# Self attention of the first stage: another order of its work, heads in alternating halves, the context copy ahead of the reciprocal root

## The reference

```python
x = x + _L0_xattn_ref(_layernorm(x, axis=-1), ctx_768, Wq, Wk, Wv, Wo, bo)

# inside, with h = 8 heads of d = 64
q = (x @ Wq).reshape(B, Sq, h, d).transpose(0, 2, 1, 3)
k = (context @ Wk).reshape(B, -1, h, d).transpose(0, 2, 1, 3)
v = (context @ Wv).reshape(B, -1, h, d).transpose(0, 2, 1, 3)
scores = jnp.einsum('bhid,bhjd->bhij', q, k) * d ** (-0.5)
attn = jax.nn.softmax(scores, axis=-1)
out = jnp.einsum('bhij,bhjd->bhid', attn, v)
out = out.transpose(0, 2, 1, 3).reshape(B, Sq, h * d)
return out @ Wo + bo
```

## Time and profile before

| | us |
|---|---|
| median of three executions | 5142.15 (5141.17 to 5146.36) |
| the profiled execution | 5143.89 |
| its span, first to last instruction | 5142.0 |
| mean granted TensorE clock over the span | 0.906 of full |
| stage self0, first preparation on VectorE to last residual addition | 31.92 to 407.37 |

### The profile page before, as it was taken

One profiled execution on the slowest core, in us unless ns is written; L12 is line 12 of the kernel. 1 busy time (PEld: TensorE's weight loads), 2 busy tenths in 40 slices (PEclk: granted clock), 3 DMA queues, 4 the chain that ended last, 5 costly groups with the idle time before them and its releaser, 6 DMA issues. The chain is left out here.

```text
span 5142.0 us, 72988 instructions
## 1 busy us (share of the span) xinstructions
PE 4271.9 (83%) x23248; PEld 3274.5 (64%) x23248; DVE 3517.8 (68%) x8249; ACT 2240.1 (44%) x5337; POOL 492.5 (10%) x921
## 2 busy tenths in 40 slices
PE   6993588799879999999999999999514787787786
PEld 5771477577647777777777777778302555555554
DVE  4656666666667777777777777777754777777445
ACT  2331366455436555555555555655240222222322
POOL 0002100101130000000000000000301121121300
PEclk9995799899979999999999999999655888888689
DMA  2000000000000000000000000000002000000101
GB/s 59 0 0 22 33 0 0 1 0 0 12 6 1 4 1 4 3 2 4 2 4 2 4 2 4 2 2 1 3 11 59 0 0 0 0 0 0 36 0 33
DMA packets 33742, 41.23 MB, mean 8 GB/s; under 512 B 5116, under 2 KB 29954, under 8 KB 33414
## 3 DMA queue, kind: packets, MB, share of 16 engines
q1 hardware_dynamic: 33480, 38.08, 2.5%
HBM read 33.61 MB, written 4.19 MB: 7 GB/s over the span
## 5 line engine op out<-in xcount | busy, mean ns | idle before, releaser
L1563 DVE TENSOR_TENSOR global_prob_t_low<-psum,global_prob_t_high 128x512 fp32r<-128x512 f32 x960 | 657.1, 690 | 252.2 <-ACT global_prob_t_high L1655 238.0
L1655 ACT ACTIVATE global_prob_t_high<-psum 128x512 fp32r<-128x512 f32 x960 | 569.9, 601 | 586.9 <-PE psum L1769 586.9
L1569 DVE TENSOR_REDUCE global_top<-psum 128x1 f32<-128x480 f32 x1024 | 666.1, 657 | 109.2 <-PE psum L1729 104.2
L1676 ACT ACTIVATE global_prob<-psum,global_bias 128x480 f32<-128x480 f32 x1024 | 674.2, 662 | 17.9 <-DVE global_bias L1572 15.1
L1769 PE MATMUL psum<-ident,global_prob 128*128 128x128 f32 x3840 | 568.3, 273 | 37.1 <-DVE global_prob_t_low L1563 36.1
L1769 PEld LDWEIGHTS psum<-ident,global_prob 128*128 128x128 f32 x3840 | 467.4, 141 | 196.1 <-DVE global_prob_t_low L1563 68.7
L1727 PE MATMUL psum<-global_prob_t_high,global_v_low 128*128 128x512 f32 x960 | 455.7, 475 | 0.9
L1727 PE MATMUL psum<-global_k_high,global_q_low 128*128 128x480 f32 x1024 | 390.2, 381 | 15.6 <-ACT global_prob L1676 13.1
L1729 PE MATMUL psum<-global_k_high,global_q_high 128*128 128x480 f32 x1024 | 391.3, 382 | 0.0
L1728 PE MATMUL psum<-global_k_low,global_q_high 128*128 128x480 f32 x1024 | 388.3, 379 | 0.0
L1728 PE MATMUL psum<-global_prob_t_low,global_v_high 128*128 128x512 f32 x960 | 379.4, 395 | 0.0
(11 more groups left out here) (439 smaller groups left out, 8147.2 us busy)
## 6 DMA issues: line engine op xcount, KB each, us to landing
x_res<-in_x SPq DMA_DIRECT2D x4, 1024.0 KB, 9.6
moe_we<-in_expert_t SPq DMA_DIRECT2D x8, 512.0 KB, 7.6
out<-x_res SPq DMA_DIRECT2D x4, 1024.0 KB, 8.7
cho_wqkv<-in_L_ffn_Wqkv SPq DMA_DIRECT2D x2, 1536.0 KB
self_ctx_t<-in_ctx_t SPq DMA_DIRECT2D x2, 1440.0 KB
sel_w<-in_L_xattn_W SPq DMA_DIRECT2D x2, 1024.0 KB, 11.9
global_ctx_t<-in_ctx_t SPq DMA_DIRECT2D x1, 1440.0 KB
sel_ctx_t<-in_ctx_t SPq DMA_DIRECT2D x1, 1440.0 KB
```

The lines of the kernel that those rows point to most:

```text
L1563: dve.tensor_tensor(dst, psum, high.bitcast(F32), ALU.subtract).then_inc(ready.sem, 1)
L1569: ins = dve.tensor_reduce(top[:, c:c + 1], w.psum[:, c, 0:chunk], AX.X, ALU.max)
L1655: act.activation(dst, psum, ACT.Copy).then_inc(ready.sem, 1)
L1676: act.activation(prob[:, par, j, c * chunk:(c + 1) * chunk], w.psum[:, c, 0:chunk], ACT.Exp, bias=bias[:, j % 2:j % 2 + 1], scale=scale, a ...
```

## The change

attention_stage, which had many options, is removed; wide_heads_stage, written for 8 heads of 64, takes its place. What differs in the work:

- Scores and attention go through the pairs, and within a pair through both heads, so that halves of the array alternate.
- The transposed xn and the queries get banks of their own (6 and 7). TensorE no longer waits for the subtraction before the xn transposes; the scores wait for the subtraction of the turn before.
- TensorE's order: scores, transposes of probabilities, xn transposes, K or V, attention, queries, bias and output. The wait for the residual addition stands before the second half of the transposes.
- The queries are copied by ScalarE instead of VectorE. ScalarE's order: probabilities, xn, exponential, attention, queries, keys or values. The keys are one instruction instead of four.
- GpSimd copies the context ahead of the reciprocal root.
- The bias matmul has 128 rows, of which all but 2 are zero; they are cleared once.

```diff
 GpSimd, in a turn
-                    if exists(3):
-                        layernorm_rstd(pool, w, chain, t + 3, 1 - s)
                     if s == 0 and exists(2):
                         if exists(0):
                             pool.wait_ge(v_psum.sem, v_psum.count(batch))
                         pool.tensor_copy(ctx_b[:, :, :], ctx_t[:, :, batch + 1, :]).then_inc(ctx_copied.sem, 1)
+                    if exists(3):
+                        layernorm_rstd(pool, w, chain, t + 3, 1 - s)
 VectorE
-        bo_parts = sb("bo_parts", [2, D], F32R)
-        ones_r = sb("ones_r", [2, P], F32R)
+        bo_parts = sb("bo_parts", [P, D], F32R)
+        ones_r = sb("ones_r", [P, P], F32R)
+                dve.memset(bo_parts[:, :].bitcast(F32), 0.0)
-                    if exists(2) and not softmax_is_long:
-                        keep_queries(t + 2)
 ScalarE, in a turn
                         [the two copies of the turned probabilities, as before]
-                        act.wait_ge(attn_psum.sem, attn_psum.count(t))
-                        act.activation(attn_t[:, :, :], ..., ACT.Copy).then_inc(attn_ready.sem, 1)
                         [the copy of xn, then the exponential, as before]
+                    if exists(0):
+                        act.wait_ge(attn_psum.sem, attn_psum.count(t))
+                        act.activation(attn_t[:, :, :],
+                                       w.psum[:, attn_bank, 0:parts * P].rearrange("p (k t) -> p k t", t=P),
+                                       ACT.Copy).then_inc(attn_ready.sem, 1)
+                    if exists(2):
+                        act.wait_ge(q_psum.sem, q_psum.count(t + 2))
+                        act.activation(q_t[:, :, :],
+                                       w.psum[:, q_bank, 0:parts * P].rearrange("p (k t) -> p k t", t=P),
+                                       ACT.Copy).then_inc(q_ready.sem, 1)
                     if s == 0 and exists(2):
                         act.wait_ge(k_psum.sem, k_psum.count(batch + 1))
-                        for k in range(parts):
-                            last = act.activation(k_t[:, k, :], w.psum[:, 3, k * NCTX:(k + 1) * NCTX],
-                                                  ACT.Identity, bias=bk[:, k:k + 1] if biased else 0.0)
-                        last.then_inc(k_ready.sem, 1)
+                        act.activation(k_t[:, :, :], w.psum[:, k_bank, 0:parts * NCTX]
+                                       .rearrange("p (k j) -> p k j", j=NCTX),
+                                       ACT.Copy).then_inc(k_ready.sem, 1)
```

More of the change, by code:

```diff
@@ L3018, in chosen_attention_stage @@
         "x_updated")})
-load_self0, self0 = attention_stage("self0", 8, 64, "L0_xattn_Wq", "L0_xattn_Wk", "L0_xattn_Wv", "L0_xattn_Wo",
-                                    "L0_xattn_bo")
+load_self0, self0 = wide_heads_stage("self0", "L0_xattn_Wq", "L0_xattn_Wk", "L0_xattn_Wv", "L0_xattn_Wo",
+                                     "L0_xattn_bo")
 load_self1, self1 = narrow_heads_stage("self1", "L1_xattn_w_q", "L1_xattn_w_k", "L1_xattn_w_v",
```

495 lines of the change are left out of this document (215 added, 280 removed).

## The result

The changed kernel takes 5066.7 us in the median of four executions (5064.39 to 5070.99), against 5141.68 for the kernel before on the same chip. The ratio is 0.9853, with a 95% interval of 0.9838 to 0.9869. The forecast was 5070.0. The profiled execution took 5068.76 us with a span of 5067.0, which is 75.0 less than the span of before.

A forecast was written before the change was run, and what follows sets the result against it. TensorE was taken to bound the first stage. 15 pairs of turns saving 4.47 us each, plus 4.7 and 0.4 at the ends, made 72.2 off 5142.15: 5070.0 us, range 5057 to 5090.

The forecast's parts named there:

- What bounds the stage: First stage, self0: TensorE bounds it, busy for 315.06 of 337.49 us, with VectorE busy for 201.42.
- Pairing: Scores and attention: alternating halves leave 8 steps each; scores 1.08 instead of 1.63 us, attention 1.02 instead of 1.52.
- The rule that was weighed against attention's pairing: Attention: weight loads overlap matmuls only in different row groups, so column halves would not pair and attention keeps 1.52 us.
- The waits: TensorE's 1.00 us before K goes through GpSimd's new order; about half a microsecond before attention is covered by other work.
- The term that was mis-sized: Queries group on TensorE, put at 1.88 us in each turn's sum.
- The ends: Stage's start and end: first transposes near 51.35, 4.7 us sooner; the end takes 13.4 us instead of 13.8.
- The sum: Whole stage: 15 pairs x 4.47 = 67.1 us, plus 4.7 at the start, plus 0.4 at the end: 72.2.
- The new small wait: Each turn: query, key or attention copy ends late; 0.5 us in each of 32 turns costs 16: 5086; chance 0.16.
- That attention or scores don't pair: TensorE's halves don't overlap: attention alone 16 us less gain, 5086; scores too, 5104; chance 0.08.
- That something else sets the turn: A serial loop of scores, softmax and output sets the turn; only the first turn's gain is left, 5137; chance 0.03.
- The clock, held to be the slower side's mechanism: Reordered stage at 1.2 GHz part of the time: about 9 us longer per turn, whole stage 5358; chance 0.03.

The follow-up runs named there:

- the two swaps: The changed kernel with scores, and in a second run attention, back in the old order (all first heads, then all second): 5090.65 us and 5095.57 us.
- the kernel with the root first: The changed kernel with GpSimd's order undone, the reciprocal root ahead of the context copy: 5161.97 us, ratio 1.0026 to the kernel before.
- the one with both changes: The kernel before with attention alternating between the two heads of a pair and GpSimd copying the context first: 5125.99 us, ratio 0.9963.

## Why the prediction was right, point by point

**What bounds the stage.** Three of the forecast's readings of rows 3 are off by 0.01 (attention 1.51, K 1.89, queries 1.88), which changes nothing. Right: TensorE was the bound and, with every wait covered, still is. Each edit of its work moved the turn by what the edited groups gained or lost, up and down, and moves of work between VectorE and ScalarE did not.

**Pairing.** Right in mechanism and size: 1.09 and 1.02 against 1.08 and 1.02, both undone one by one. The rule that was weighed against attention's pairing, from the Trainium skill, TensorE: Matmul & The Clock Gate, The mechanism (Part 3), doesn't hold here: with shared row groups 16 loads and 16 matmuls fit in 1.02 us, in which the loads are busy for 0.85 and the matmuls throughout.

**The waits.** Right in place. The forecast said that without its cover the wait ahead of attention would be back with half a microsecond; paired attention in the old order shows it, with 1.83 instead of 1.34. What the forecast did not price is the cover of GpSimd's copy: it gave the gain of that move inside the sum (the 1.2 of the K turn) and never what the new TensorE order would cost without it. It is 6.1 a pair, more than the whole gain of 4.65: 3.16 of wait and 2.9 of work at the lower clock. K had been moved ahead of the attention that filled its wait.

**The term that was mis-sized.** The queries were put at 1.88, the old size, though part of it was the stop ahead of a bias matmul of 2 rows, which the same paragraph removes. They take 1.81; with the 2 rows back, 1.98. With 0.01 to 0.02 on bias and output, this makes the pair 18.03 in the forecast and 17.84 measured, 15 x 0.18 = 2.7 us.

**The ends.** The first transposes start at 51.30 (forecast 51.35):

```profile
45.12 0.44 PE L203 MATMUL psum<-ident,self_xn 128*128 128x128 f32 x2
```

The wait of 2.44 there is gone. Something else went with it that the forecast doesn't have. In the kernel before, the clock fell behind that wait, and V took 3.21 instead of 1.72:

```profile
48.29 3.42 PE L869 MATMUL psum<-self_wv,self_ctx_b 96*120 96x512 f32 x4
...
48.29:51.50 3.21, 3.21 (x6) 1.17 (x5) 1.82 (x4) 1.27 (x2) 0.73 (x2) 0.53 0.00 0
```

The queries and the scores stood behind it, so about 1.5 of the 4.8 us gained at the start are the clock's. The forecast still came out right, because it took the new start from VectorE's chain, which is what the first transposes now wait for.

The end takes 12.38, where 13.4 was forecast and 13.82 it was. The forecast took off 0.7 because attention's copy stands behind the exponential. The delay is there (copy at 322.41, right behind it), but it isn't on the path: the last transposes wait for the product of the softmax and start 6.18 behind those of tile 30, where they had started 7.45 behind them, after a wait of 1.48 that the residual addition ended last.

```profile
322.41 0.58 ACT L380 ACTIVATE self_attn_t<-psum 128x512 f32<-128x512 f32 x1
...
323.96 1.16 DVE L345 TENSOR_TENSOR self_prob<-self_prob,self_total 128x960 f32<-128x960 f32 x1
...
325.18 1.15 PE L423 MATMUL psum<-ident,self_prob 128*120 128x128 f32 x8
```

In the kernel before:

```profile
401.00 1.09 PE L838 MATMUL psum<-ident,self_prob 128*120 128x128 f32 x8 [1.48 <-DVE x_res L773]
```

**The sum.** Middle 69.8 (forecast 67.1), start 4.8 (4.7), end 1.4 (0.4): the stage's work ends 76.0 earlier. From the first load of the next stage on, the profiled execution is 1.0 longer than that of before, hence 75.0. That 1.0 has nothing to do with the change; it is luck that it brought the sum nearer to the forecast.

**The rivals.** The new small wait did not come. That attention or scores don't pair is refuted by the two swaps. That something else sets the turn is refuted by the same. The clock, held to be the slower side's mechanism, did not act in the changed kernel, where TensorE has no wait in steady turns and the granted clock is 1.00 from the first transposes to the stage's end; yet it is the right mechanism. It had acted at the start of the kernel before. It acts in the kernel with the root first, and from where I had looked away: I argued that idle gaps get shorter everywhere, which is true only because of the copy's new place.

## What to carry to other kernels

Where small matmuls use half of the array, write them so that the halves alternate, and put other work between them and the copy that feeds them; pairing attention alone gained nothing here, while pairing the scores, which waited for no copy, gained its full 0.54 a turn. When a matmul group is moved ahead of work that covered its wait, look for the instruction that it waits for, and for what is queued ahead of that on its engine: here a copy of 0.38 us behind a root of 0.8, which itself waits for VectorE's statistics, decided over some 90 us. Price each part of a change also as if it were left out, since parts that enable each other are not worth their sums.

## What the runs showed of the hardware that was not expected

The clock can make a wait cost twice. After an idle stretch of 3.0 us the granted clock was 0.50 in the K turn shown, and 2.9 us of slow work came on top; with 2.2 us of useless work put into the stretch, which left an idle 0.81, K ran at its usual speed and the stage was 42.1 us shorter. An idle stretch of 2.44 us at the start of the kernel before was followed by V at 0.53. Idle stretches of 0.74 and 0.99 us with 1.5 of work between them had the same effect in 4 of 15 K turns; 0.25 and 1.00 in the kernel before, and 0.74 alone in the one with both changes, had it in none. Stretches of 0.83 and 1.03 at the stage's end had it in the kernel with the queries copied by VectorE and not in the changed one. Short waits like these can lower the clock and often don't; what decides isn't shown.

A bias matmul that isn't there doesn't give back its time: with it, queries to output took 2.01 us, without it 1.89, though the bias itself stood there with 0.20. Where the other 0.08 went isn't shown.

The same code of the other stages, from the first load of the next stage on, lasted from 4729.1 to 4749.3 us in the profiled executions of the fourteen kernels. A difference of the whole time within this spread of 20 us can therefore lie outside this stage; the stage's own timeline tells, and where the clock stays up it repeats to about 0.01 us from turn to turn.
